# A relative-position attention kernel: band product of 130 columns, its constant end written from one column, and one turn of the row maxima per step

## The reference

```python
qkv = q @ in_proj_weight.T + in_proj_bias            # split in heads; qh = qh / sqrt(d)
scores = einsum('bhid,bhjd->bhij', qh, kh)
rel    = clip(pos[None, :] - pos[:, None], -K, K) + K          # 0 .. 128
bias_r = einsum('bhid,rd->bhir', qh, rel_pe)                   # rel_pe: (129, 16)
bias   = take_along_axis(bias_r, rel, axis=-1)
attn   = softmax(scores + bias, axis=-1)
out    = einsum('bhij,bhjd->bhid', attn, vh) @ out_w.T + out_b
x = layernorm(x + out); x = layernorm(x + ffn(x))
```

## Time and profile before

| | |
|---|---|
| median of 3 runs | 2427.24 us (2426.69 to 2430.31) |
| the profiled execution, its own time | 2427.77 us |
| its span | 2426.1 us |
| granted PE clock, mean | 0.975 |
| PE, DVE, ACT, POOL busy in the span | 93%, 72%, 69%, 40% |

### The profile page before, as it was taken

One profiled execution on the slowest core, in us unless ns is written; L12 is line 12 of the kernel. 1 busy time (PEld: TensorE's weight loads), 2 busy tenths in 40 slices (PEclk: granted clock), 3 DMA queues, 4 the chain that ended last, 5 costly groups with the idle time before them and its releaser, 6 DMA issues. The chain is left out here.

```text
span 2426.1 us, 47764 instructions
## 1 busy us (share of the span) xinstructions
PE 2266.8 (93%) x14642; PEld 1273.6 (52%) x14642; DVE 1742.5 (72%) x3444; ACT 1669.9 (69%) x2239; POOL 964.5 (40%) x1565
## 2 busy tenths in 40 slices
PE   4998599999999999999999999999999999799997
PEld 3555244444444444444444444444444444688886
DVE  2444467777777777777777777777777773588885
ACT  2443167777777777777777777777777777466766
POOL 0000444443444434443344433444334432466663
PEclk8999589999999999999999999999999999899999
DMA  6998777777777777777777777767767762333321
GB/s 179 357 335 317 216 186 204 204 209 207 204 207 200 208 207 204 203 205 205 204 204 204 209 207 202 204 201 208 210 199 207 201 196 88 104 99 108 108 63 44
DMA packets 335292, 468.58 MB, mean 193 GB/s; under 512 B 90517, under 2 KB 263270, under 8 KB 335206
## 3 DMA queue, kind: packets, MB, share of 16 engines
q0 software_dynamic: 120960, 215.78, 34.9%
q1 hardware_dynamic: 201206, 243.05, 30.1%
q10 hardware_dynamic: 13040, 8.80, 1.2%
HBM read 244.73 MB, written 221.25 MB: 192 GB/s over the span
## 5 line engine op out<-in xcount | busy, mean ns | idle before, releaser
L903 ACT ACTIVATE probs<-weigh_ps 128x1024 f32<-128x1024 f32 x1024 | 1048.8, 1025 | 403.7 <-PE weigh_ps L1069 400.4
L955 DVE CUSTOM_DVE_ANT_1 ring_ps<-ring_ps,band_all 128x512 f32<-128x512 f32 x1008 | 681.0, 715 | 265.9 <-PE ring_ps L1029 265.7
L1029 PE MATMUL ring_ps<-keys,queries 48*128 48x512 f32 x2048 | 839.2, 474 | 32.2 <-DVE partial_max L944 10.4
L1069 PE MATMUL weigh_ps<-queries,keys 50*128 50x512 f32 (+3 forms) x2688 | 752.7, 386 | 1.4 <-ACT probs L903 1.1
L944 DVE TENSOR_REDUCE partial_max<-ring_ps 128x2 f32<-128x1024 f32 x512 | 627.7, 1226 | 155.3 <-PE ring_ps L1029 115.0
L1029 PEld LDWEIGHTS ring_ps<-keys,queries 48*128 48x128 f32 x2048 | 370.6, 187 | 511.1 <-issue 394.5
L1086 PE MATMUL sum_ps<-probs,values 128*32 128x512 f32 x4096 | 547.3, 606 | 0.1
L1054 PE MATMUL weigh_ps<-ident,band_all 128*128 128x128 f32 x2048 | 362.7, 290 | 23.2 <-ACT carried L891 20.3
L1069 PEld LDWEIGHTS weigh_ps<-queries,keys 50*128 50x128 f32 x2688 | 356.7, 186 | 17.7 <-ACT probs L903 9.5
L790 POOL DMA_DIRECT2D band_all<-band_scr x320 | 230.6, 723 | 331.4 <-DMA band_scr<-carried 319.6
L1054 PEld LDWEIGHTS weigh_ps<-ident,band_all 128*128 128x128 f32 x2048 | 214.0, 141 | 246.2 <-ACT probs L903 104.6
(11 more groups left out here) (115 smaller groups left out, 1861.3 us busy)
## 6 DMA issues: line engine op xcount, KB each, us to landing
band_scr<-carried SPq DMA_DIRECT2D x256, 512.0 KB, 4.1
band_all<-band_scr POOLq DMA_DIRECT2D x128, 512.0 KB, 6.6
band_all<-band_scr POOLq DMA_DIRECT2D x128, 256.0 KB, 3.3
keys<-k_scr POOLq DMA_DIRECT2D x128, 240.0 KB, 9.0
k_scr<-k_parts SPq DMA_DIRECT2D x16, 1792.0 KB, 8.2
q_scr<-q_parts SPq DMA_DIRECT2D x16, 1024.0 KB, 6.2
queries<-q_scr POOLq DMA_DIRECT2D x128, 128.0 KB, 2.9
o_scr<-weighted_s SPq DMA_DIRECT2D x64, 256.0 KB, 9.1
```

The costliest lines, as they stand in the source:

```text
L903: nc.scalar.activation(probs[:, u % PROBS], weigh_ps[weigh_of["scores", at]][:], ACT.Exp).then_inc(s_pr, 1)
L955: nc.vector.tensor_tensor_reduce(out=both, in0=both, in1=bias, scale=1.0, scalar=LOWEST, op0=ALU.add, op1=ALU.max, accum_out=partial_max[: ...
L1029: nc.tensor.matmul(dst, query_rows(c, h, ROWS, tile * P, (tile + 1) * P), key_rows(c, h, ROWS, c0, c0 + 512), start=True, stop=True, tile_ ...
L1069: last = nc.tensor.matmul(weigh_ps[weigh_of["scores", at]][:, h, e0 * P:e1 * P], key_rows(c, h, QROWS, k0, k0 + P), query_rows(c, h, QROWS ...
```

## The change

It does two things.

1. The band product of tiles 0 to 6 writes `NARROW` = 130 columns for each head in place of 256. Columns 128 to 255 all hold the same product (the last relative position). ACT writes them from column 128 alone: `copy_band` becomes two ACTIVATEs of 2 x 128 columns, of which the second reads one column with a step of zero. Tile 7 stays as it was.
2. The row maxima of both halves of a step are negated, split, turned, copied and sent together at u = 10; nothing is turned at u = 4. POOL's three operations run once on 16 elements a partition, PE's transpose gives 32 rows, and SP sends two DMAs of 2 x 1024 columns in place of four of 2 x 512. The buffers are laid out anew for that, and the semaphores count once a step. Which of two heads is looked at first in unit 4 changes with it.

```diff
+            NARROW = P + 2
-            TURN_AT = {4: 0, 10: 1}
+            TURN_AT = 10
             def turns_at(step, u):
-                return u in TURN_AT and 0 <= step + 1 < G
+                return u == TURN_AT and 0 <= step + 1 < G
...
-                def load_minus_max(i, step, g):
+                def load_minus_max(i, step):
                     c = step + 1
-                    sp.wait_ge(s_tc, cnt(i, 2, 2 * c + g + 1))
+                    sp.wait_ge(s_tc, cnt(i, 1, c + 1))
...
-                def minus_maxima(i, step, g):
+                def minus_maxima(i, step):
                     c = step + 1
-                    done = cnt(i, 2, 2 * c + g + 1)
-                    pool.wait_ge(s_rm, done)
-                    nc.gpsimd.tensor_tensor(negative[:, g], zero[:], row_max[:, g], ALU.subtract)
+                    pool.wait_ge(s_rm, cnt(i, 2, 2 * c + 2))
+                    nc.gpsimd.tensor_tensor(negative[:], zero[:], row_max[:], ALU.subtract)
...
-                    if 0 <= step + 1 < G:
-                        minus_maxima(i, step, 0)
                     read_chunk(i, step, 0)
...
                     if 0 <= step + 1 < G:
-                        minus_maxima(i, step, 1)
+                        minus_maxima(i, step)
...
-                    nc.scalar.activation(band_out[:, chunk % BANDS_OUT, :, e], weigh_ps[weigh_of["band", n]][:, :, 0:2 * P],
+                    product, kept = weigh_ps[weigh_of["band", n]], band_out[:, chunk % BANDS_OUT, :, e]
+                    if n % NT == NT - 1:
+                        nc.scalar.activation(kept, product[:, :, 0:2 * P], ACT.Copy).then_inc(s_be, 1)
+                        return
+                    nc.scalar.activation(kept[:, :, 0:P], product[:, :, 0:P], ACT.Copy)
+                    end = product[:, :, P]
+                    nc.scalar.activation(kept[:, :, P:2 * P], flat(end, 0, [end.ap[0], end.ap[1], [0, P]]),
                                          ACT.Copy).then_inc(s_be, 1)
...
-                        table = rel_terms[h * ROW_TILE:h * ROW_TILE + ROWS, :].rearrange("p (a c) -> p a c", a=3)
-                        moving = table[:, 0:3:2] if tile == NT - 1 else table[:, 0:2]
+                        table = rel_terms[h * ROW_TILE:h * ROW_TILE + ROWS, :]
+                        product, moving = dst[:, h, 0:NARROW], table[:, 0:NARROW]
+                        if tile == NT - 1:
+                            product = dst[:, h, 0:2 * P].rearrange("p (a c) -> p a c", a=2)
+                            moving = table.rearrange("p (a c) -> p a c", a=3)[:, 0:3:2]
```

More of the change, by code:

```diff
@@ L577, in post_ln_block @@
             partial_max = sb("partial_max", [P, 2, HG, QT, 2], F32)
[L578 to L582, removed]
+            row_max = sb("row_max", [P, HG, 2, QT], F32)
+            negative = sb("negative", [P, HG, 2, QT], F32)
+            negative_parts = sb("negative_parts", [P, HG, PARTS, 2, QT], F32)
+            zero = sb("zero", [P, HG, 2, QT], F32)
+            minus_max = sb("minus_max", [HG * PARTS * NT, P], F32R)
             weighted_s = sb("weighted_s", [P, 2, 512], F32)
@@ L607, in post_ln_block @@
             s_tc = sem("minus_max_copied")
-            s_min = [[sem(f"minus_max_in{g}_{a}") for a in range(SLOTS)] for g in range(2)]
+            s_min = [sem(f"minus_max_in{a}") for a in range(SLOTS)]
             s_sc = sem("scores_ready")
@@ L634, in turn_index @@
             def turn_index(step, u):
-                return 2 * (step + 1) + TURN_AT[u]
+                return step + 1
             def weighed(m):
@@ L721, in write_bands @@
                                  ).then_inc(s_bw[n % BANDS_OUT], 16)
-                def load_minus_max(i, step, g):
+                def load_minus_max(i, step):
                     c = step + 1
-                    sp.wait_ge(s_tc, cnt(i, 2, 2 * c + g + 1))
+                    sp.wait_ge(s_tc, cnt(i, 1, c + 1))
                     for h in range(HG):
                         r0 = h * ROW_TILE + ROWS
[L728 to L731, removed]
+                        rows = queries[r0:r0 + PARTS, c % SLOTS, :].bitcast(F32)
+                        sp.dma_start(rows.rearrange("r (a p) -> r a p", a=NT),
+                                     minus_max[h * PARTS * NT:(h + 1) * PARTS * NT, :].bitcast(F32)
+                                     .rearrange("r (a p) -> r a p", a=1)).then_inc(s_min[c % SLOTS], 16)
                 def store_sums(i, c):
@@ L740, in unit @@
                     if turns_at(step, u):
-                        load_minus_max(i, step, TURN_AT[u])
+                        load_minus_max(i, step)
                     if u == 5 and step > 0:
@@ L993, in wait_for @@
                         elif kind == "turn":
-                            pe.wait_ge(s_tc, cnt(i, 2, n + 1))
+                            pe.wait_ge(s_tc, cnt(i, 1, n + 1))
                         elif kind == "scores":
@@ L1014, in band_product @@
                     for h in range(HG):
-                        table = rel_terms[h * ROW_TILE:h * ROW_TILE + ROWS, :].rearrange("p (a c) -> p a c", a=3)
-                        moving = table[:, 0:3:2] if tile == NT - 1 else table[:, 0:2]
-                        last = nc.tensor.matmul(dst[:, h, 0:2 * P].rearrange("p (a c) -> p a c", a=2),
-                                                query_rows(c, h, ROWS, tile * P, (tile + 1) * P), moving,
+                        table = rel_terms[h * ROW_TILE:h * ROW_TILE + ROWS, :]
[3 more added lines that the diff above has]
+                            moving = table.rearrange("p (a c) -> p a c", a=3)[:, 0:3:2]
+                        last = nc.tensor.matmul(product, query_rows(c, h, ROWS, tile * P, (tile + 1) * P), moving,
                                                 start=True, stop=True, tile_position=(h * ROW_TILE, 0))
@@ L1033, in turn_max @@
                 def turn_max(i, n):
-                    g = n % 2
-                    pe.wait_ge(s_mm, cnt(i, 2, n + 1))
+                    pe.wait_ge(s_mm, cnt(i, 1, n + 1))
                     dst = ring_bank(i, ("turn", n))
-                    nc.tensor.transpose(dst[0:HG * PARTS * QT, 0:P],
-                                        negative_parts[:, g].rearrange("p h c t -> p (h c t)"),
+                    nc.tensor.transpose(dst[0:HG * PARTS * NT, 0:P],
+                                        negative_parts[:].rearrange("p h c g t -> p (h c g t)"),
                                         ident[:]).then_inc(s_turn, 1)
```

14 lines of the change are left out of this document (7 added, 7 removed).

## The result

| | median | against before |
|---|---|---|
| before | 2428.58 us (2426.69 to 2430.31, 4 runs) | |
| the change | 2408.66 us (2408.09 to 2410.89, 4 runs) | 0.9921 [0.9908, 0.9934] |

The change makes the kernel 19.9 us faster. I had forecast 6.4 us, to 2420.8, with a range of 2415.5 to 2427.5. The sign was right, the size three times too small, and the time lies outside the range. The profiled execution took 2409.02 us, span 2407.3 (before: 2427.77 and 2426.1).

The account below looks back on a forecast made before the run. The prediction took handovers between PE and ACT, not PE's 93% busy share, as the bound. Its terms summed to -0.10 us a step, times 62 is -6.2, with 0.2 for the prologue -6.4: 2420.8 us, range 2415.5 to 2427.5.

Parts of the forecast that it names:

- The turn at u = 4 goes.: Pair 2: the removed turn ran while PE waited for the band copy, and scores 1 wait for exponentials anyway; worth nothing.
- The sign for pair 3: Pair 3: time from weighted matmuls to scores 1 was to grow by 0.05 to 1.18 us, still behind the exponentials.
- The narrow product's record: Band product on PE (line 1024): its narrow form was to be some 50 ns shorter.
- Band product in pairs 0 and 4: Pairs 0 and 4, where scores 1 wait for the weighted matmuls: the shorter product gives -0.05 us each.
- No gain where the exponentials come last: Pairs 1, 3, 6 and 7: scores 1 wait for exponentials, so a shorter band product gives nothing there.
- In pair 1 I had +0.02: Pair 1: weighted matmuls start 0.05 us earlier, but PE waits for the split copy, +0.07; net +0.02 us.
- In pair 2 I had -0.02: Pair 2: the shorter product gains only -0.02 us, for the little room before its exponentials bind.
- my four terms: Per step: pair 0 -0.05, pair 1 +0.02, pair 2 -0.02, pairs 4 and 5 -0.05; sum -0.10 us.
- The later turn at u = 10: Pair 5: scores 0 and their exponentials start 0.02 us later, absorbed by 0.13 us of room before scores 1.
- rival 4: Split copy on ACT, pair 1: reading one column runs at half rate, +0.21 us, step +0.11, 2434 us; chance 0.11.
- I had 0.28 and 0.66: Split band copy on ACT: the two copies start 0.28 us apart and end 0.66 us after the first's start.
- my +0.07: POOL's part of the u = 10 turn: 16 elements add 0.024 us to each of three operations, +0.07 us.

Follow-up runs that it names:

- experiment 2: Kernel after the change with the narrow band product and split copy undone, leaving one turn a step at u = 10: 2417.00 us, 0.9958 of before.
- experiment 3: Kernel before, with ACT's copy of the u = 4 turn moved to pair 1, ahead of the exponentials of scores 1, all work kept: 2419.46 us, 0.9965.
- experiment 4: Kernel before, with the narrow band product and split copy in tiles 2 and 3 alone (pairs 6 and 7): 2426.31 us, 0.9991.
- experiment 7: Kernel before, with only the band copy split in two ACTIVATEs, the second reading one column: 2431.30 us, 1.0014.
- experiment 1: Kernel before, with the narrow band product and split copy alone, both turns kept: 2421.63 us, 0.9969.
- experiment 9: Kernel before, with ACT's band copy ahead of the weighted sums in pair 1: 2408.35 us, 0.9934 of before.
- experiment 5: Changed kernel, with ACT's band copy ahead of the weighted sums in pair 1: 2373.55 us, 0.9787 of before.

## Why the prediction was wrong

**The step that failed** is "*The turn at u = 4 goes.* ... Nothing." I saw that the look behind it waited for ACT's copy, and followed that wait only to the next thing on PE: band product and weighted matmuls of pair 2, which would come earlier and then wait for the exponentials. That part is true (experiment 2, pairs 1 and 2). I did not follow the look to its reader. DVE's reduction came late with it, and the ring slot that it frees was due one unit later, for a look that stands ahead of the bias transposes of pair 3. Experiment 3 shows it with all work kept: -0.12 us a step for moving one copy. With -0.13 for this step in place of 0 the sum would have been -0.23, and 62 times that is -14 us, which my range would still not have held (2413). The sign for pair 3 was wrong as well. I expected 1.18 us from weighted to scores 1 there, but its product stays wide, so nothing could lengthen it, and it fell to 1.02.

**The terms that held.** The narrow product's record is 53 ns shorter (290 ns in the mean, below, against 343), for a forecast of 50. Band product in pairs 0 and 4, -0.05 each: -0.06 and -0.05. No gain where the exponentials come last: experiment 4. In pair 1 I had +0.02 (copy +0.07, earlier weighted matmuls -0.05) and it came to -0.02, since the copy cost +0.05 (experiment 7) and the rest gave -0.07. In pair 2 I had -0.02 and it gave nothing. So the band part came to -0.13 where my four terms had -0.10. The later turn at u = 10 was absorbed (0 in columns 4 and 5 for one turn alone).

The groups by line and form of the changed kernel, for the narrow product, the copies and POOL:

```profile
L1024 PE MATMUL weigh_ps<-rel_terms,queries 48*128 48x130 f32 x896 | 145.9, 290 | 18.4 <-DMA queries<-q_scr 17.3 <-ACT carried L895 0.9
...
L893 ACT ACTIVATE carried<-weigh_ps 128x256 f32<-128x256 f32 x448 | 169.5, 378 | 48.1 <-PE weigh_ps L1024 48.1
...
L895 ACT ACTIVATE carried<-weigh_ps 128x256 f32<-128x256 f32 x448 | 175.5, 392 | 0.0
...
L815 POOL TENSOR_TENSOR negative_parts<-negative,negative_parts 128x16 f32<-128x16 f32 x64 | 14.0, 218 | 5.0
```

and the two copies in pair 1, from its timeline of ACT:

```profile
1215.70 0.38 ACT L893 ACTIVATE carried<-weigh_ps 128x256 f32<-128x256 f32 x1
1215.96 0.39 ACT L895 ACTIVATE carried<-weigh_ps 128x256 f32<-128x256 f32 x1
```

The copy that reads one column of each head 128 times costs about what the copy of 2 x 128 columns costs (392 and 378 ns), so rival 4 falls. The two start 0.26 us apart and end 0.65 after the first's start; I had 0.28 and 0.66. POOL's three operations grew by 3, 5 and 16 ns in their records, 0.024 us together and not each. But their starts also moved apart: in experiment 2 the last of them ends 0.05 us later behind the weighted matmuls of pair 4 (2.02 against 1.96, medians of 54 steps), near my +0.07, and the turn starts 0.035 later. In the changed kernel the turn starts 2.12 us behind weighted (1224.25 to 1226.37) against 2.03 before. The rest of that is the weighted matmuls, which now come sooner: experiment 1, with POOL's work as before, has 0.04 of it.

**Rules weighed.** Weighted follows the product 0.06 us sooner, 0.26 against 0.32. My estimate from the sustained figures of the Trainium skill, "TensorE: Matmul & The Clock Gate", section "Back-to-back issue gap", was 16 ns; the measurement decides against it here. The estimate of 93 ns for one more ACTIVATE, from the Trainium skill, "ScalarE: Activation LUTs", section "What ACT_TABLE_LOAD costs", stands against +0.05 us a step in experiment 7; here too the measurement decides.

**The part outside the steps.** 62 x 0.24 = 15 us leaves about 5 of the 19.9, for which my forecast had 0.2. The two profiled spans, 2426.1 and 2407.3 us, differ by 18.8. Of that, 3.3 us lie before the first exponentials, 2.5 in step 0 (34.2 us before, 31.7 with the change, from its first exponentials to those of step 1), 11.2 in the 62 steps with the stall in them, and 1.8 behind.

For most of step 0's 2.5 us the profiles show a cause. In the kernel before, PE waited 2.03 us at 329.95 for the turn, because POOL stood 13.3 us at a band read ahead of the row maxima. From 331.6 us on the granted clock was 0.5 (1.2 GHz) for 3.4 us, and the eight weighted matmuls there took 1.80 us in place of 1.07. In the changed kernel POOL stood there 13.0 us, but PE's wait was 0.92 us and the clock stayed at 1.0 (2.4 GHz). Step 0 took 34.2 to 35.6 us in the five profiles with such a fall in it (before, experiments 1, 3, 7, 9), and 30.1 to 32.7 in the six without. Experiment 4, which has both turns, is without it and has 31.7. All five kernels with one turn a step are without it too. So it may be that one turn a step spares step 0 this fall more often, but one profile of each kernel does not show that. How much of the 5 us is the change's stays open.

## What to carry to other kernels

To follow a wait along its own engine is not enough: ask also who reads what the waiting instruction makes, and what that reader frees. A small copy that stands on ACT behind a long instruction can hold a buffer for several engines in a row; moving one of 0.25 us ahead gave 8 us without any work removed (experiment 3). And where two copies are due at one place, the one with a waiting reader goes first: on the changed kernel that was worth 0.59 us a step, more than the whole change (0.24), and with that order in both kernels the change brought 0.53 (experiments 5 and 9).

## What the runs showed of the hardware

One stall shows how far a late DMA reaches. In step 4 of the changed kernel's profile POOL waited for a band write before it came to the row maxima, and PE for these (timelines of POOL and PE):

```profile
434.72 0.78 POOL L804 DMA_DIRECT2D band_all<-band_scr  x1 [7.82 <-DMA band_scr<-carried]
```

```profile
436.27 0.28 PE L1042 MATMUL ring_ps<-ident,negative_parts 128*32 128x128 f32 x1 [2.06 <-POOL negative_parts L815]
```

The step took 30.5 us in place of 27.2. The wait is 2.06 us of that. The rest comes with a slower clock: behind the wait the granted clock fell from 1.0 to 0.5 (2.4 to 1.2 GHz) at 437.8 us and was back at 1.0 at 441.2, and the next eight weighted matmuls took 1.85 us in place of 1.07. The eleven profiles show eight such falls inside attention (between 310 and 2000 us of the span), each right behind a wait of PE for the turn of 2.03 to 3.53 us. PE's other waits there were 1.0 us or less, and none of them was followed by a fall. So a late transfer cost PE twice, once by the wait and once by the slower clock.

POOL's order puts a read that may be late ahead of three short operations that PE needs; the kernel before has the same order at u = 10.
